# The last tap of a four-tap convolution, multiplied by ScalarE instead of VectorE

## What is computed

```python
z = x @ W_mem                                   # 512 -> 256 + 32 columns
z = lax.conv_general_dilated(z, conv_k, window_strides=(1,), padding=[(CONV_W - 1, 0)],
        dimension_numbers=('NHC', 'HIO', 'NHC'), feature_group_count=MEM + K)   # CONV_W = 4
k_val, s_raw = z[..., :MEM], z[..., MEM:]
p_w = jnp.exp(jnp.clip(score_scale * s_raw, -20.0, 20.0) + log_w)
phi = k_val[..., None] * theta                  # 8 angles for each of the 256
num_re, num_im = cumsum(p_w * cos(phi)), cumsum(p_w * sin(phi))   # over the rows; den = cumsum(p_w)
```

## Time and profile before

| | |
|---|---|
| median of 3 runs | 1212.84 us (1212.49 to 1217.21) |
| the profiled execution | 1213.98 us, of which the span from first to last instruction is 1212.6 us |
| PE busy | 1038.2 us, 86% of the span |
| DVE busy | 729.8 us, 60% |
| ACT busy | 647.4 us, 53% |
| POOL busy | 483.2 us, 40% |
| granted TensorE clock, mean | 0.940 |

### The profile page before, as it was taken

One profiled execution on the slowest core, in us unless ns is written; L12 is line 12 of the kernel. 1 busy time (PEld: TensorE's weight loads), 2 busy tenths in 40 slices (PEclk: granted clock), 3 DMA queues, 4 the chain that ended last, 5 costly groups with the idle time before them and its releaser, 6 DMA issues.

```text
span 1212.6 us, 11351 instructions
## 1 busy us (share of the span) xinstructions
PE 1038.2 (86%) x3424; PEld 570.9 (47%) x3424; DVE 729.8 (60%) x1210; ACT 647.4 (53%) x1104; POOL 483.2 (40%) x451
## 2 busy tenths in 40 slices
PE   5887999868899889899879979985987899979993
PEld 3454544534445554334545434442554644436661
DVE  2320017698899899689969978994996931200000
ACT  4343334488546685445775675344588851414441
POOL 3454522353525542431632414521483431155542
PEclk9988999989999989899879989987999999989997
DMA  9876662666735866653856754353785763225666
GB/s 315 303 238 157 117 147 61 166 156 114 156 112 135 216 159 124 166 140 92 234 123 132 180 121 128 100 147 79 161 192 119 153 112 63 69 79 99 114 109 104
DMA packets 68978, 172.54 MB, mean 142 GB/s; under 512 B 12355, under 2 KB 12355, under 8 KB 66791
## 3 DMA queue, kind: packets, MB, share of 16 engines
q0 software_dynamic: 32576, 72.44, 33.2%
q1 hardware_dynamic: 36342, 99.38, 26.6%
HBM read 112.86 MB, written 68.33 MB: 149 GB/s over the span
## 4 chain that ended last, share of the span: by engine, by line
PE 31%; ACT 7%; DMA 5%; issue 3%; DVE 3%; POOL 1%; SPq 1%; DVEq 0%; ACTq 0%; POOLq 0%
PE hps L854 7%; PE yps L870 6%; PE misc L932 5%; PE yps L812 5%; PE hps L800 4%; DMA outT<-tail_sb 2%; DMA out_rows<-ys,into_i 1%; DMA x_rows<-ys,rows_i 1%; ACT L1036 1%; ACT ys L1049 1%; ACT hidden_sb L1036 1%; PE misc L923 1%; SPq L1855 1%; PE xps L923 1%; PE xps L845 1%
## 5 line engine op out<-in xcount | busy, mean ns | idle before, releaser
L870 PE MATMUL yps<-w_all,hidden_sb 128*128 x424 | 213.9, 629 | 39.7 <-ACT hidden_sb L1036 39.5
L854 PE MATMUL hps<-w_all,hidden_sb 128*128 x848 | 219.0, 404 | 25.3 <-ACT hidden_sb L1036 16.4
L1641 POOL DMA_INDIRECT xs<-x_normal,rows_i x106 | 124.1, 1171 | 216.2 <-PE xps L845 164.7
L854 PEld LDWEIGHTS hps<-w_all,hidden_sb 128*128 128x128 f32 x848 | 166.1, 202 | 80.7 <-issue 60.8
L1441 DVE TENSOR_TENSOR_SCAN run<-pwx,trig 128x512 f32<-128x512 f32 x128 | 149.3, 1207 | 24.8 <-ACT trig L1124 24.4
L1665 POOL DMA_INDIRECT x_rows<-ys,rows_i x56 | 101.6, 1813 | 105.5 <-ACT ys L1049 99.1
L870 PEld LDWEIGHTS yps<-w_all,hidden_sb 128*128 128x128 f32 x424 | 81.3, 200 | 117.8 <-issue 115.1
L1049 ACT ACTIVATE ys<-yps,slots 128x512 f32<-128x512 f32 x106 | 73.0, 689 | 110.9 <-PE yps L870 90.4
L800 PE MATMUL hps<-xnT,sw_sb 128*128 128x512 f32 x256 | 120.9, 621 | 6.5 <-ACT hidden_sb L1009 6.5
L812 PE MATMUL yps<-sw_sb,hidden_sb 128*128 128x512 f32 x256 | 120.8, 615 | 0.0
L1627 POOL DMA_INDIRECT slots<-told,dest_i x64 | 75.3, 1176 | 54.0 <-DVE cmp_a L1310 30.3
(11 more groups left out here) (202 smaller groups left out, 1531.1 us busy)
## 6 DMA issues: line engine op xcount, KB each, us to landing
qx<-q_cols SPq DMA_DIRECT2D x128, 256.0 KB
w_all<-in_w_experts SPq DMA_DIRECT2D x8, 1024.0 KB, 10.3
x_normal<-xin SPq DMA_DIRECT2D x32, 256.0 KB, 4.6
xin<-x_rows SPq DMA_DIRECT2D x32, 256.0 KB, 6.7
turns_sb<-in_w_out SPq DMA_DIRECT2D x3, 1536.0 KB, 13.7
xin<-in_x SPq DMA_DIRECT2D x16, 256.0 KB, 5.3
sum_rows<-ys SPq DMA_DIRECT2D x16, 256.0 KB, 3.0
xin<-sum_rows POOLq DMA_DIRECT2D x16, 256.0 KB, 8.2
```

What stands on the lines that cost most here:

```text
L854: t = PE.matmul(hps[:, bank, 0:H], xT[:, j % 2, c, :], w_all[:, bass.ds(expert[j] + c * H, H)], start=c == 0, stop=c == KC - 1)
L870: t = PE.matmul(yps[:, bank, :], hb[:, j % 2, ec, :], w_all[:, bass.ds(expert[j] + (KC * H + ec * D), D)], start=ec == 0, stop=ec == EC - 1)
L1641: GE.indirect_dma_start(xs[:, j % NX, :], None, xn_rows[PAIR_OF[g]], bass.IndirectOffsetOnAxis(rows_i[:, g % 2, j:j + 1], 0)).then_inc(*xs ...
```

## The change

The last tap (line 1372) leaves VectorE. A new ScalarE stage `last_tap`, in the order under the name "a_mem", reads the PSUM bank and writes the product with the weight column to the same target, as an activation Copy with a scale for each partition. It takes over the waits of the old instruction (TensorE's product; for `kval` the phases that last read the slot) and adds two that VectorE had by its own order: for the score tile the denominators of the batch before, and in the first batch the weights of line 1542. VectorE's first remaining tap waits for a new semaphore `tapped`. The planner is told of an ACT stage of cost 0.7 that follows PE, and a DVE stage of 2.3 instead of 3.0 that follows ACT. The bank is still freed by the last tap of line 1375. No matmul, no transfer and no tile is added or removed.

```diff
-                piece("DVE", s, 3.0, ("PE", s))
+                piece("ACT", s, 0.7, ("PE", s))
+                piece("DVE", s, 2.3, ("ACT", s))
...
-        convolved = signal("s_convolved", [(*s, j) for s in staged("a_mem", "DVE") for j in range(CW)])
+        convolved = signal("s_convolved", [(*s, j) for s in staged("a_mem", "DVE") for j in range(1, CW)])
+        tapped = signal("s_tapped", staged("a_mem", "ACT"))
...
+            def last_tap(b, i):
+
+                at = slice(0, P) if i < HALVES else slice(K, 2 * K)
+                act.wait_ge(*mem_made.at((b, i)))
+                if i < HALVES and HALVES * b + i >= NK:
+                    act.wait_ge(*phase_made.at(divmod((HALVES * b + i - NK) * M + M - 1, STEPS)))
+                if i == HALVES and b:
+                    act.wait_ge(*den_made.at((b - 1, 3)))
+                if i < HALVES and not b:
+                    act.wait_ge(*weighing.at(21))
+                SE.activation(kept(b, i) if i < HALVES else s_row, misc[at, misc_turn.at["a_mem", b, i][0], :], ACT.Copy,
+                              scale=conv_sb[at, i, CW - 1:CW]).then_inc(*tapped.of((b, i)))
...
+                elif stage == "a_mem":
+                    last_tap(*at)
...
-                vec.wait_ge(*mem_made.at((b, i)))
-                if i < HALVES and HALVES * b + i >= NK:
-                    vec.wait_ge(*phase_made.at(divmod((HALVES * b + i - NK) * M + M - 1, STEPS)))
-                VE.tensor_scalar(o, z, conv_sb[at, i, CW - 1:CW], None, ALU.mult).then_inc(*convolved.of((b, i, 0)))
+                vec.wait_ge(*tapped.at((b, i)))
                 for j in range(1, CW):
-                    vec.wait_ge(*convolved.at((b, i, j - 1)))
+                    if j > 1:
+                        vec.wait_ge(*convolved.at((b, i, j - 1)))
```

## The result

The changed kernel takes 1226.61 us (median of 6 runs, 1224.35 to 1228.40), the kernel before, run beside it, 1215.35 us (6 runs, 1212.49 to 1218.29). The ratio is 1.0115, 95% interval 1.0079 to 1.0151: 14 us slower, give or take 4 (the two medians as they stand are 11.3 us apart). The forecast was 1210.9 us with a range of 1204 to 1218, and the likeliest outcome "no change". It was wrong.

What follows compares the result with a forecast made beforehand. TensorE holds 31% of the chain and sets the pace after attention; VectorE holds 3%. Terms 0.78 + 0.39 + 0 + 0.77 = 1.9 us take the median from 1212.84 to 1210.9 us, range 1204 to 1218.

Steps and rivals of the forecast that it cites:

- What can't be read from the trace: Remade order of all engines' lists: 5 us allowed either way, from four table loads or one longest cosine wait.
- The direct effect: Twelve convolutions: 0.78 + 0.39 + 0 + 0.77 = 1.9 us won, between +0.1 us and -6.2 us.
- The new instruction: Last tap on ScalarE: 0.689 us each, as line 1049; a rival estimate from the skill's ratio was about 2.2 us.
- Batches 0 and 1: Six convolutions: zero won, covered by VectorE's waits of 6.26 and 3.21 us for a transfer, which grow longer.
- Batch 2: Three convolutions: 0.77 us won, between 0 and 2.3; most becomes a cosine wait of about 2.6 us near 590 us.
- Batch 3, i = 0: Convolution on the chain at 788.4 us: ScalarE is idle when the product ends, so 0.78 us are won.
- Batch 3, i = 1: Convolution on the chain at 801.0 us: the tap may wait behind ScalarE's trigonometry; 0.39 us won, between -0.86 and +0.78.
- The signs of being wrong: Table loads or line 1441's waits moving over 5 us, or VectorE ending its steps over 6 us off 973 us.
- The reading of the bound: After attention TensorE sets the pace, busy 61.79 of 62 us; earlier gains count only if its work closes up.
- (A): Attention: VectorE paces all of it and remade lists close gaps; 6.2 to 9.4 us won, 1203.4 to 1206.6 us; chance 0.24.
- (B): Whole run: nothing reaches the end, gains become waits for ScalarE and full TensorE swallows the rest; 1212.8 us; chance 0.20.
- (C): ScalarE's list: tap ahead of trigonometry waits for its product; three places cost 10.8 us, 1221.7 us; chance 0.13.

Runs made afterwards that it cites:

- e2_old_orders: The change's work with the lists of all five engines as planned for the kernel before; ratio to the kernel before 0.9995 (0.9965 to 1.0024), 1214.91 us.
- e14_tap_early: The change's work with the lists of the kernel before, the tap 3.7 us ahead of its product's planned end; ratio to the kernel before 1.0177, 1232.78 us.
- e1_slots_back: The changed kernel with ("slots", 3) put back behind ("c_out", 1, 0) in SyncE's list; ratio to the kernel before 1.0083, 1227.09 us.
- e3_new_orders: The work of the kernel before with the lists planned from the change's costs (0.7 on ScalarE, 2.3 on VectorE); ratio to the kernel before 1.0156, 1233.15 us.
- e4_slots_ahead: The kernel before with ("slots", 3) moved ahead of ("c_out", 1, 0) in SyncE's list; ratio to the kernel before 1.0056, 1223.64 us.
- e13_two_ahead: The kernel before with ("slots", 3) moved ahead in SyncE's list, ("x", 3, 0) and ("one", 3, 0) in TensorE's and ScalarE's; ratio 1.0078, 1220.84 us.
- e5_two_places: The changed kernel with ("slots", 3) put back in SyncE's list, ("x", 3, 0) and ("one", 3, 0) in TensorE's and ScalarE's; ratio to the kernel before 1.0163, 1230.70 us.

## Why the prediction was wrong

**The step that failed** is the one headed "What can't be read from the trace". It saw that twelve costs change in the planner and that every later choice can fall otherwise, and then gave this term 5 us, by two sizes that lie at hand: four table loads, or the longest wait for the cosine. Measured, the term is 0.2 to 2.3% of the run, that is 2 to 28 us, and 14 to 19 us for the change's own costs. It was wrong in two ways. The size: a place in a list is priced by what stands behind it in the queue (at one place a move issued 6.3 us later and 9.45 us of TensorE), and many places move at once. And the centre: the prediction let it fall either way alike, and of eight kernels with remade lists none was faster. It had 0.02 for "slower by the order alone"; the whole result went there.

**The direct effect** was put at 1.9 us, between +0.1 and -6.2. e2_old_orders has -0.6 us (1215.66 x 0.0005) with an interval from 4.3 us won to 2.9 us lost. So the sum of 1.9 us is neither shown nor refuted; of the parts the trace of e2_old_orders tells this:

```profile
231.94 0.69 DVE L1227 BATCH_NORM_STATS2 stats_ffn<-xin 128x6 f32<-128x512 f32 x1 [6.28 <-DMA xin<-in_x]
...
404.84 1.33 DVE L1227 BATCH_NORM_STATS2 stats_ffn<-xin 128x6 f32<-128x512 f32 x2 [4.12 <-DMA xin<-in_x]
...
800.29 0.67 ACT L1135 ACTIVATE kval<-misc,small_sb 128x512 f32<-128x512 f32 x1
...
800.99 2.32 DVE L1396 SCALAR_TENSOR_TENSOR kval<-misc,small_sb,kval 128x511 f32<-128x511 f32 x3 [1.42 <-ACT kval L1135]
```

- *The new instruction*: 0.67 to 0.69 us here, 0.68 to 0.72 in the changed kernel, as estimated from its neighbour. The estimate of 2.2 us after the Trainium skill ("ScalarE: Activation LUTs", section "Rules for kernel authors") was out by a factor of three for f32 out of PSUM.
- *Batches 0 and 1*: the waits for the transfer are 6.28 and 4.12 us where they were 6.26 and 3.21. The cover is still there, and one of the two waits is longer, as foretold.
- *Batch 2*: the prediction expected a wait for the cosine of over 2 us near 590 us. With the old lists none appears; the scans at 580.99 and 585.82 us wait for nothing. What the 2.3 us of this batch came to isn't shown.
- *Batch 3, i = 0*: VectorE's first tap of line 1375 began at 789.22 us, 1.50 us after the instruction ahead of it had begun at 787.72; with the tap on ScalarE it begins at 787.74, 0.71 us after its own forerunner. That is 0.79 us won, as foretold.
- *Batch 3, i = 1*: the first tap on VectorE now begins after a wait of 1.42 us for ScalarE, which makes the trigonometry first, as foretold from the earlier trace rows. It begins at 800.99 us, 0.75 us earlier than before; after i = 0 the lead was 1.48 us. So 0.73 us were given back here, and the 0.39 us that the sum counts for i = 1 as won didn't come; that is within the ends given, near the lower.
- *VectorE and ScalarE busy*: VectorE's busy time fell by 8.2 us with the old lists (721.6), by 7.3 with the new, foretold 8.9. ScalarE's rose by 6.9 and 4.9 us, foretold 8.3; with the new lists two table loads of 1.283 us are gone.

**The signs of being wrong** came, two of the three. The number of table loads hardly moved (129 to 127), but the waits at line 1441, now 1456, went from 24.4 us in 15 to 33.6 us in 20:

```profile
DVE run L1456 <- ACT trig L1139: 33.6, 20, 4.2
```

```profile
980.75 1.41 DVE L1501 SCALAR_TENSOR_TENSOR tail_sb<-outT,small_sb,misc 128x512 f32<-128x512 f32 x2 [1.36 <-PE misc L913]
```

The last scaled half of VectorE came at 980.75 us and not near 973. What the prediction didn't name was TensorE's own idle time and SyncE's queue; of the 13.5 us more of idle time on TensorE 13.3 lie from 500 to 570 us.

**The reading of the bound** held in one part: TensorE, full after attention, sets the end. It cuts the other way than it was used. Idle time that TensorE collects earlier is handed to the end, as work left over. From 1030 us on it is busy 163.5 us in the changed kernel and was 147.2 us before, 16.3 us more. Its idle time there shrank by 4.9 us, where the wait of 7.28 us for gathered rows at 1085.34 us is gone; the rest is the 11.4 us of the span.

**The rivals.** (A) fell: even without any last tap, with the lists of before, the gain is at most 0.4%, and no remade list brought one. (B), nothing reaches the end, is what e2_old_orders looks like, with the lists held still. (C) gave a time near the measured one, 1221.7 us, by the wrong cause: ScalarE's waits in place before the tap are 19.9 us in the changed kernel and 17.2 in e2_old_orders, which loses nothing. e14_tap_early shows what the mechanism costs once the tap stands too early.

**What stays open.** Which of the hundreds of moved stages carry the 14 to 19 us of the change's lists isn't known beyond one, the place of ("slots", 3), worth about 7 us in the lists of before. Undone in the changed kernel it gave back nothing that the trace shows, so the costs of places don't simply add up. Why the order before is better than its neighbours isn't explained by any single stretch either: the places of the loss differ from list to list. The other long wait of the changed kernel's stretch, 7.96 us for ScalarE's rows at 506.54 us (1.90 us at 507.06 us before), wasn't taken apart; it is still 7.65 us in e1_slots_back. Whether the order before had been chosen among others by its time, which would let its neighbours look worse, isn't known. To give one engine alone another list wasn't tried. No version was found that beats the kernel before; e2_old_orders equals it.

## What to carry to other kernels

Where a planner inside a kernel makes the order of all queues from a table of costs, an edit of a cost is an edit of everything, and its price can be many times what the moved work is worth (here 14 to 19 us, against a direct effect between 4.3 us won and 2.9 us lost). Price it apart: run the new work with the old order, the old work with the new order, and the old work with the cost disturbed by a few per cent; this last gives the spread that every prediction has to carry, and here it was all on the slow side. And before a stage is put on a queue in order, ask what is ready behind it: behind one fetch that waited for GpSimd a finished half was issued 8.0 us after it was ready, where it had been 3.5, and taps placed one product too early cost 21 us.

## What the runs showed of the hardware

- TensorE's busy time for the same 3424 matmuls ran, in the kernels of the table, from 1027.3 us (e2_old_orders, mean granted clock 0.945) to 1044.6 us (e3_new_orders, 0.934), and from 500 to 570 us, the stretch with the gaps, the clock was 0.83 (e3_new_orders and the changed kernel) against 0.95 before. Idle time on TensorE is thus not all of the loss in e3_new_orders: 11.9 us more idle and 6.4 us more busy.
- One instruction of GpSimd's scatter to the same place took 4.80 us in the kernel before (at 511.35 us) and 6.97 us in the changed one (at 510.92 us), as the profile gives it. It is 4.80 or 4.81 us in all four profiles looked at that have the lists of before or nearly so (before, e2_old_orders, e4_slots_ahead, e13_two_ahead), and 6.97 or 6.98 us in all four with the change's lists (the changed kernel, e1_slots_back, e3_new_orders, e5_two_places). What slows it wasn't tried.
